# Late scatters of trees 1 and 2 issued during the FFN's first quads, with longer TensorE filler and earlier zero fills, in an attention + routed FFN kernel

## What is computed

```python
x = x + _L0_xattn_ref(_layernorm(x), ctx_1024, ctx_1024, w_q, w_k, w_v, w_o)
x = x + _L0_ffn_ref(_layernorm(x), ...)

def _fff(x, node_w, node_b, w1, b1, w2, b2):
    cur = jnp.zeros((N,), jnp.int32)
    for _ in range(DEPTH):                      # 4
        score = jnp.einsum('nd,nd->n', xf, node_w[cur]) + node_b[cur]
        cur = 2 * cur + 1 + (score >= 0).astype(jnp.int32)
    sel = jax.nn.one_hot(cur - N_NODES, N_LEAVES)      # 16 leaves
    hidden = relu(jnp.einsum('nd,ldh->lnh', xf, w1) + b1[:, None, :]) * sel.T[:, :, None]
    return jnp.einsum('lnh,lho->no', hidden, w2) + sel @ b2

q = _fff(x, q_...); k = _fff(x, k_...); v = _fff(x, v_...)
attn = softmax(einsum('bqd,bkd->bqk', q, k) / sqrt(256));  return attn @ v
```

## Time and profile before

| | |
|---|---|
| median of 3 runs | 658.25 us (657.19 to 658.79) |
| span of the profiled execution | 692.2 us |
| granted TensorE clock, mean | 0.941 |
| TensorE busy | 602.4 us, 87% |
| VectorE, ScalarE, GpSimd busy | 437.1, 297.2, 236.4 us |
| DMA | 173.78 MB, 251 GB/s on average |
| scatters (96 indirect DMAs) | 95.5 us busy, 995 ns each |
| first quad's transposes start | 440.77 us |
| last `copy_y` of the FFN starts | 601.25 us |

### The profile page before, as it was taken

One profiled execution on the slowest core, in us unless ns is written; L12 is line 12 of the kernel. 1 busy time (PEld: TensorE's weight loads), 2 busy tenths in 40 slices (PEclk: granted clock), 3 DMA queues, 4 the chain that ended last, 5 costly groups with the idle time before them and its releaser, 6 DMA issues.

```text
span 692.2 us, 14814 instructions
## 1 busy us (share of the span) xinstructions
PE 602.4 (87%) x5131; PEld 501.3 (72%) x5131; DVE 437.1 (63%) x1511; ACT 297.2 (43%) x482; POOL 236.4 (34%) x298
## 2 busy tenths in 40 slices
PE   7668999998998999999989766699968879787997
PEld 6556888887777878887778556588736747676995
DVE  3854677888788888898888746544403423154664
ACT  4114454454444444454444420277625625632322
POOL 5700011332422333234232435400266264355341
PEclk9869999999999999999999988599969978999999
DMA  6897989899989999999884887599958977755552
GB/s 191 254 304 226 276 260 256 262 274 284 290 241 286 299 264 275 292 298 288 242 273 141 275 244 184 190 325 340 395 174 291 340 245 248 255 162 170 167 172 87
DMA packets 105015, 173.78 MB, mean 251 GB/s; under 512 B 14128, under 2 KB 73200, under 8 KB 104944
## 3 DMA queue, kind: packets, MB, share of 16 engines
q1 hardware_dynamic: 93088, 146.03, 67.7%
q0 software_dynamic: 9216, 25.18, 11.8%
q10 hardware_dynamic: 2640, 1.65, 0.9%
HBM read 92.59 MB, written 79.69 MB: 249 GB/s over the span
## 4 chain that ended last, share of the span: by engine, by line
PE 40%; DMA 18%; SPq 15%; issue 12%; DVE 6%; another core or an unknown queue 4%; ACT 4%; ACTq 1%; POOL 0%; DVEq 0%; POOLq 0%
DMA parts_dram<-k_lo 9%; SPq L330 7%; DMA parts_dram<-q_hi 6%; PE banks L819 5%; PE banks L808 5%; PE banks L834 5%; PE banks L876 3%; PE banks L897 3%; PE banks L539 3%; PE banks L524 3%; SPq L316 2%; PE banks L551 2%; DMA k<-parts_dram 2%; PE banks L865 2%
## 5 line engine op out<-in xcount | busy, mean ns | idle before, releaser
L1526 POOL DMA_INDIRECT xs_dram<-xn2s,place x96 | 95.5, 995 | 174.8 <-ACT pt L928 144.6
L928 ACT ACTIVATE pt<-banks 128x768 f32<-128x768 f32 x128 | 103.5, 810 | 114.3 <-PE banks L552 92.9
L1166 DVE TENSOR_REDUCE mneg<-banks 128x2 f32<-128x512 f32 x240 | 121.8, 549 | 48.3 <-PE banks L540 42.6
L539 PE MATMUL banks<-k,q 107*128 107x256 f32 x240 | 76.1, 368 | 22.3 <-DMA k<-parts_dram 12.8
L551 PE MATMUL banks<-q,k 109*128 109x256 f32 x256 | 74.1, 341 | 2.0 <-DMA q<-m_lo 0.3
L539 PEld LDWEIGHTS banks<-k,q 107*128 107x128 f32 x240 | 46.2, 193 | 33.9 <-DMA k<-parts_dram 17.4
L1383 DVE COPY wb<-tables 128x128 f32 x96 | 21.4, 223 | 73.2 <-remote 44.4
L567 PE MATMUL banks<-pt,vp 128*32 128x256 f32 (+1 forms) x1024 | 56.8, 341 | 5.4 <-ACT pt L928 5.4
L552 PE MATMUL banks<-q,k 109*128 109x128 f32 x256 | 57.5, 224 | 0.0
L808 PE MATMUL banks<-ident,xb 128*128 128x128 f32 x288 | 42.8, 295 | 14.2 <-issue 11.0
L540 PE MATMUL banks<-k,q 107*128 107x128 f32 x240 | 54.2, 226 | 0.0
(11 more groups left out here) (177 smaller groups left out, 1301.8 us busy)
## 6 DMA issues: line engine op xcount, KB each, us to landing
ys_dram<-yb SPq DMA_DIRECT2D x36, 512.0 KB
xb<-xs_dram SPq DMA_DIRECT2D x35, 512.0 KB
k<-parts_dram SPq DMA_DIRECT2D x128, 128.0 KB
q<-parts_dram SPq DMA_DIRECT2D x128, 128.0 KB
xs_dram<-zero SPq DMA_DIRECT2D x45, 256.0 KB
parts_dram<-q_hi SPq DMA_DIRECT2D x32, 256.0 KB
xs_dram<-zero SPq DMA_DIRECT2D x18, 384.0 KB, 4.5
tables<-leafw SPq DMA_DIRECT2D x16, 257.0 KB
```

The lines of the kernel that those rows point to most:

```text
L539: mm(ps[:, 0:S], q[0:KN, t, P:S], k[0:KN, t, :], start=True, stop=True)
L928: nc.scalar.activation(pt[:, 2 * p:2 * p + 2, :], st_banks(b, p)[:, :, 0:S + P], ACT.Exp, scale=SC).then_inc(exp_sb, 1)
L1166: last = nc.vector.tensor_reduce(mneg[1 - u][:, t, 2 * j:2 * j + 2], S_BANKS[:, :, cols], axis=AX.X, op=ALU.max, negate=True)
L1526: gp.indirect_dma_start(xs_dram[tree], bass.IndirectOffsetOnAxis(ap=place[:, k:k + 1], axis=0), xn2s[m % RING][:, t, :], None).then_inc(sc ...
```

## The change

- Batch 11's six scatters are issued one at a time in step 15, at the slots of `SLOTS`, each behind one more exponential (counts 119 to 124). Batch 12's into tree 0 comes at j = 7 of step 15, those of batches 13, 14 and 15 into tree 0 at j = 2 of steps 16, 17 and 18.
- The 16 indirect DMAs of batches 12 to 15 into trees 1 and 2 are issued after the pipeline, one about every two thirds of a quad, tied in turn to `xbT_ps`, `y_ps` and `h_ps`, from quad 0 to quad 10. GpSimd then waits that they have landed, ahead of its gathers. SP waits for tree 1's before it loads quad 12 and for tree 2's before quad 24.
- Since the ring has three slots, batch 15's normalised rows go to `vp[0]`, which attention no longer uses; VectorE waits for `pv_ps` there in place of batch 12's scatters.
- The zero fills 16, 17 and 18 are issued in step 15 straight after that of 15, twelve DMAs in a row, and counted in `zeroed_last`.
- The filler between the leaf matmul and `block_T(0)` has 90 matmuls for 24.

Only the last filler's count differs. The diff:

```diff
@@ -192,7 +192,7 @@
         ident_ok, ones_ok, wq_in, wk_in = (sem(n) for n in "ident_ok ones_ok wq_in wk_in".split())
         wt_late = sems("wt_late", TREES)
         x_in, c_in, xr_in = sems("x_in"), sems("c_in"), sems("xr_in")
-        zeroed_first, zeroed = sem("zeroed_first"), sems("zeroed")
+        zeroed_first, zeroed, zeroed_last = sem("zeroed_first"), sems("zeroed"), sem("zeroed_last")
         (stats1, aggr1, var1, rstd1, xn_done, xnT_ps, xnT_sb, q_ps, qh_sb, ql_sb, k_ps, kh_sb, kl_sb,
          v_ps, v_sb, s_ps, max_sb, mT_ps, mh_sb, ml_sb, st_ps, exp_sb, pv_ps, nd_sb, ndT_ps, rden_sb, a_sb, aT_ps, aT_sb,
          wo_ps, x1_sb, stats2, aggr2, var2, rstd2, xn2_sb, xn2T_ps, xn2T_sb, node_ps, sc_sb,
@@ -254,6 +254,12 @@
 
             eng.wait_ge(scat[tree][m % RING], 16 * T * (m // RING + 1))
 
+        def xn2_rows(m):
+
+            if m < NB - 1:
+                return xn2s[m % RING]
+            return vp[0][:].rearrange("p t h c -> p (t h c)")[:, 0:T * D].rearrange("p (t d) -> p t d", t=T)
+
         def lag(b):
 
             return LAG + 1 if b < NB - 1 else LAG
@@ -276,7 +282,7 @@
 
         NCONST = 3
         WARM, FILL, FILL_K, FILL_X = 36, 6, 24, 8
-        IDLE = 14, 24, 30, 8, 16, 70, 24
+        IDLE = 14, 24, 30, 8, 16, 70, 90
         NALC = 11
 
         S_BANKS, ST_BANKS, W_BANKS, G6, G7 = pairs[0], pairs[1], banks[4:6], banks[6], banks[7]
@@ -333,15 +339,10 @@
             def zero_pages(b):
 
                 k = 3 if b <= 3 else 2
-                done = zeroed_first if b <= 3 else zeroed[b % 2]
+                done = zeroed_first if b <= 3 else zeroed_last if b >= NB else zeroed[b % 2]
                 for tree in range(TREES):
                     sp.dma_start(by_page(xs_dram[tree])[:, zero_from(b):zero_from(b + 1), :],
                                  zero[:, 0:k * D].rearrange("p (r d) -> p r d", d=D)).then_inc(done, 16)
-
-            def zero_after(b):
-
-                sp.wait_ge(zeroed[b % 2], 16 * TREES * ((b - 4) // 2))
-                zero_pages(b)
 
             def load_table(t, k):
 
@@ -377,10 +378,11 @@
                     stack(b + 1, 1 - u, 3)
                 if has(b, 2):
                     unload(b + 2, n + 1, u, 0)
-                if b <= NB:
+                if b < NB:
                     zero_pages(b)
-                if b == NB + 1:
-                    zero_after(b + 1)
+                if b == NB - 1:
+                    for late in (NB, NB + 1, NB + 2):
+                        zero_pages(late)
                 if has(b, -1):
                     load_xr(b - 1, 1 - u)
                 if has(b, -2):
@@ -409,8 +411,6 @@
                         sp.wait_ge(st_ps, PAIRS * (NB - 1))
                         for k in range(2):
                             load_table(1 if b <= NB else 2, (b - NB + 1) % 2 * 2 + k)
-                    if b == NB:
-                        zero_after(b + 1)
 
             def ramp():
                 for b in range(2):
@@ -455,6 +455,9 @@
 
             def load_quad(q):
 
+                if q % QUADB == 0:
+                    for m in range(NB - RING, NB):
+                        scattered(sp, q // QUADB, m)
                 ge(sp, xbT_ps, q - QB + 1)
                 rows = quad_rows(xs_dram[q // QUADB], q % QUADB)
                 if q == 0:
@@ -468,16 +471,10 @@
                 sp.wait_ge(y_sb, q + 1)
                 sp.dma_start(quad_rows(ys_dram[q // QUADB], q % QUADB), yb[q % QB][:]).then_inc(y_out[q % QB], 16)
 
-            sp.wait_ge(zeroed[0], 16 * TREES * 8)
-            sp.wait_ge(zeroed[1], 16 * TREES * 7)
-            for m in range(NB - RING, NB):
-                scattered(sp, 0, m)
-            for q in range(QB):
-                load_quad(q)
-            for tree in range(1, TREES):
-                for m in range(NB - RING, NB):
-                    scattered(sp, tree, m)
-            for q in range(QB, QB + AHEAD):
+            sp.wait_ge(zeroed[0], 16 * TREES * 6)
+            sp.wait_ge(zeroed[1], 16 * TREES * 6)
+            sp.wait_ge(zeroed_last, 16 * TREES * 3)
+            for q in range(QB + AHEAD):
                 load_quad(q)
             for q in range(TREES * QUADB):
                 if q + QB + AHEAD < TREES * QUADB:
@@ -655,7 +652,7 @@
                         for t in range(T):
                             for c in range(C):
                                 last = nc.tensor.transpose(G6[:, c * S + t * P:c * S + t * P + P],
-                                                           xn2s[(b - 2) % RING][:, t, c * P:c * P + P], ident[:])
+                                                           xn2_rows(b - 2)[:, t, c * P:c * P + P], ident[:])
                         last.then_inc(xn2T_ps, 1)
                         if b == NB + 1:
                             warm(IDLE[3])
@@ -1179,11 +1176,13 @@
 
                         v.wait_ge(rstd2, b - 1)
                         ge(v, xn2T_ps, b - 3)
-                        if b - 2 >= RING:
+                        if b - 2 == NB - 1:
+                            v.wait_ge(pv_ps, 4 * (NB - 1))
+                        elif b - 2 >= RING:
                             for r in range(TREES):
                                 scattered(v, r, b - 2 - RING)
                         for t in range(T):
-                            nc.vector.tensor_scalar(xn2s[(b - 2) % RING][:, t, :], x1[u][:, t, :], mv2[:, t, 0:1],
+                            nc.vector.tensor_scalar(xn2_rows(b - 2)[:, t, :], x1[u][:, t, :], mv2[:, t, 0:1],
                                                     rs2[:, t:t + 1], ALU.subtract, ALU.mult).then_inc(xn2_sb, 1)
                     if j == 5 and has(b, -1):
                         divide(b, 1)
@@ -1518,35 +1517,32 @@
 
                 if m == 0:
                     gp.wait_ge(zeroed_first, 16 * TREES * 6)
+                elif m + 3 >= NB:
+                    gp.wait_ge(zeroed_last, 16 * TREES * 3)
                 else:
                     gp.wait_ge(zeroed[(m + 3) % 2], 16 * TREES * ((m + 1) // 2))
                 gp.wait_ge(alloc, al(m, NAL))
                 for t in ts:
                     k = (m * T + t) * TREES + tree
                     gp.indirect_dma_start(xs_dram[tree], bass.IndirectOffsetOnAxis(ap=place[:, k:k + 1], axis=0),
-                                          xn2s[m % RING][:, t, :], None).then_inc(scat[tree][m % RING], 16)
+                                          xn2_rows(m)[:, t, :], None).then_inc(scat[tree][m % RING], 16)
 
             def step(b, n, u):
                 for j in range(PAIRS):
                     if j in SLOTS and has(b, -4) and b < NB - 1:
                         gp.wait_ge(exp_sb, PAIRS * (b - 1) + j + (LAG + 2 if j < LAG else LAG + 1))
                         scatter(b - 4, SLOTS.index(j) // T, (SLOTS.index(j) % T,))
+                    if j in SLOTS and b == NB - 1:
+                        gp.wait_ge(exp_sb, PAIRS * b - 1 + SLOTS.index(j))
+                        scatter(b - 4, SLOTS.index(j) // T, (SLOTS.index(j) % T,))
                     if j == 1 and has(b, -2):
                         rsqrt(b - 2, aggr2, mv2, ve2, var2, rs2, rstd2, (xn2_sb, T * (b - 2)))
                     if j == 2 and b >= NB:
-                        for m, tree in LAST_SCATTERS[b - NB]:
-                            scatter(m, tree)
+                        scatter(b - 3, 0)
                     if j == 4 and has(b, 3):
                         rsqrt(b + 3, aggr1, mv1, ve1, var1, rs1, rstd1, (xn_done, T * (b + 3)))
-                    if j == 6 and b == NB - 1:
-                        for tree in range(TREES):
-                            scatter(b - 4, tree)
-                        for tree in range(TREES - 1):
-                            scatter(b - 3, tree)
-
-            LAST_SCATTERS = (((NB - 4, 2), (NB - 3, 0)),
-                             ((NB - 3, 1), (NB - 3, 2), (NB - 2, 0), (NB - 2, 1)),
-                             ((NB - 1, 0), (NB - 2, 2), (NB - 1, 1), (NB - 1, 2)))
+                    if j == 7 and b == NB - 1:
+                        scatter(b - 3, 0)
 
             def ramp():
                 rsqrt(0, aggr1, mv1, ve1, var1, rs1, rstd1, (xn_done, 0))
@@ -1576,6 +1572,20 @@
 
             ramp()
             pipeline(step)
+
+            late = [(m, tree, t) for tree in range(1, TREES) for m in range(NB - RING - 1, NB) for t in range(T)]
+            for n, (m, tree, t) in enumerate(late):
+                q, third = 2 * n // 3, 2 * n % 3
+                if third == 0:
+                    gp.wait_ge(xbT_ps, q + 2)
+                elif third == 1:
+                    gp.wait_ge(h_ps, q + 1)
+                else:
+                    gp.wait_ge(y_ps, q + 1)
+                scatter(m, tree, (t,))
+            for tree in range(1, TREES):
+                for m in range(NB - RING, NB):
+                    scattered(gp, tree, m)
 
             for s in range(2):
                 gp.wait_ge(x1_out[s], 16 * (NB // 2))
```

## The result

The changed kernel took **660.49 us** (median of 19 runs, 654.75 to 667.11) beside 657.1 us before (19 runs): ratio 1.0079, interval 1.0054 to 1.0105. I had forecast 653.9 and a range of 649 to 660. It is slower, by 5.2 us (0.79% of 657.1).

A forecast was written before the change was run, and what follows sets the result against it. TensorE was taken to bound the FFN, so only the one-batch-deep seam chain, with low clock and pauses, could pay: 2.5 + 0.5 - 2.0 + 1.5 + 1.9 = 4.4 us off 658.25, giving 653.9, range 649 to 660.

The forecast's parts named there:

- The share of the pauses: Engine pauses beside rows of GpSimd's indirect DMAs: net 12.4 us gained when profiled, 0.15 of it, 1.9, when timed.
- Rival 1: The pauses are real in timed runs too, so the whole 12.4 us counts: 643.4 us; chance 0.08.
- Rival 2: About half the pauses are real, the profiled span also holding some 6 us no timed run has: 650.4 us; chance 0.10.
- `rsqrt(13)` behind two scatters: Step 15: two of batch 11's scatters ahead of `rsqrt(13)` in GpSimd's queue delay `xn2s`; 2.0 us lost.
- `rsqrt(14)` freed: Attention: `rsqrt(14)` no longer stands behind two more scatters; up to 2.4 us, taken as 1.5 gained.
- The filler: Before the first quad: 90 matmuls keep TensorE's clock high for quads 0 and 1's transposes and `block_h(0)`; 2.5 us gained.
- Rival 3: The filler buys nothing, the clock not having fallen or the 90 overshooting: say 657.3 us; chance 0.22.
- Scatters out of the seam: Seam: one or two scatters fewer lie ahead of the first quad's load; 0.5 us gained, bounds 0 to 0.7.
- 16 scatters in the FFN: Quads 0 to 10: 5.9 us of DMA work, covered by 6.4 us of ring slack; taken 0, bound 5.9.
- rival 4: The FFN becomes bound by its transfers, stores or loads landing late: slower, 661.7 us; chance 0.14.
- Zero fills: Step 15: 9 more fills on SP's queue ahead of `xr(14)` and the tables; taken 0, 1 without cover.
- My four terms beside the pauses: Filler 2.5, scatters out of the seam 0.5, `rsqrt(13)` -2.0, `rsqrt(14)` 1.5: together 2.5 us gained.

The follow-up runs named there:

- a_warm24: Changed kernel with the last filler at 24 matmuls instead of 90: 661.54 us, ratio 1.0085 to the kernel before.
- a_seam2: Changed kernel with the 16 late scatters of batches 12 to 15 back in the seam: 661.7 us, ratio 1.0104 to the kernel before (656 to 655 us kind).
- b_again2: Kernel before, unchanged, run again where it takes 655 to 657 us: 655.7 us.
- after: Profiled execution of the changed kernel, nothing else altered: span 657.5 us, time 659.62 us.
- a_again: Changed kernel, unchanged, run again where the kernel before takes 655 to 657 us: 660.65 us, ratio 1.0088 to the kernel before.
- a_wide: Changed kernel with the 90 filler matmuls of 128 columns replaced by 23 of 512 columns: 660.98 us, ratio 1.0079 to the kernel before.
- b_again: Kernel before, unchanged, run again where it takes 700 to 702 us: 704.0 us, ratio 1.0054 against itself.

## Why the prediction was wrong

I had a gain of 4.4 us; the traces beside the times show a loss of 5.9. Of the 10.3 between them 5.0 are the path from the filler to the first `copy_y`, 2.0 the scatters in the FFN, 1.9 the pauses and 1.5 the clock in step 15. The filler's term failed most in size, that of the pauses in kind.

**The share of the pauses (+1.9).** I subtracted the median of the runs from the profiled time, found 33.95 us, and read it as pauses that timed runs mostly lack, a share of 0.15. There is no share. Where the times beside the change were taken there are none, and the gain is 0; where the profile was taken, timed runs have them whole, and the change gains 8.6 us. Rival 1 put the right question, whether timed runs have them, but took the two numbers to be of one condition. With the pauses whole I had 14.9 us (2.5 and 12.4) for all terms together: measured 7.6 or 10.3 in the seam, by the two traces of before, less 2.7 in the FFN, and the profiled run of that condition spans 693.2 us, not 677.3. If the other terms cost there the 3.9 that they cost in the 655 seam, the seam's pauses were worth 11.5 to 14.2 (an estimate), not 16.1. Why a row of scatters goes with them is open.

Rival 2 leant on the Trainium skill, Runtime: NRT & Kernel Launch, "The ~15µs preamble/postamble breakdown", where a profile's total stands 6.2 us above the reported time. Here the time stands 2.1 us above the span (659.62 and 657.5).

**`rsqrt(13)` behind two scatters (-2.0).** The wait is exactly that, 1.07 to 3.05. What I left out is the clock behind it: in 388 to 394 it was granted 0.54, the transposes took 1.08 and not 0.63, and 119 to 128 lost 3.4 to 3.6. In a_warm24 and a_seam2 they waited as long but took 0.63, and it lost 2.3 and 2.0. So the term is 2.0 and up to 1.6 for the clock, which doesn't fall in every run.

**`rsqrt(14)` freed (+1.5).** Right: 1.6. VectorE's wait for `rs` ahead of `xn2s(14)` is 2.47 us in b_again2, 0.21 in the changed kernel, and 2.46 again in a_seam2, where the scatters are back.

**The filler (+2.5).** Wrong. I looked at the wait of `block_T(0)` only. With a warm TensorE `block_T(1)` is next in line, and it waits for the second quad and starts 5.9 to 7.7 us behind SP's first load. The clock doesn't last that long: the granted clock fell to 0.50 in the wait for the first quad in a_seam2, at the end of its transposes in after and a_again, and in the wait for the second in the other three, so that `block_T(1)` took 1.94 to 1.97 us in all six. What is late next I had not asked. And I costed only the filler's time, not its 132 added instructions: 1.3 to 2.1 us more to the load (5.02 to 5.82 us for 3.75 to 3.79) by the fetched block, in every trace with 90 and in none with 24 or with 23 wide ones. Rival 3 had the gain of nothing, not the loss.

**Scatters out of the seam (+0.5).** 0: the load stands 3.75 us behind the scatter with them and 3.77 without.

**16 scatters in the FFN (0, bound 5.9).** -1.7 to -2.3 in the changed kernel in the 655 condition (-4.1 in a_wide). I had compared landings with a ring of four quads. The wait that counts is in the diff: `load_quad(12)` waits for tree 1's scatters, and SP reaches it behind quad 5's store, not at quad 12. This was rival 4's mechanism in part, transfers that land late; its 661.7 came near the result by other sums. GpSimd itself was not held up: the 16 late scatters took 0.95 to 1.18 us each in after. The 3100 ns that I weighed for one was no price for this case: a copy into `wb` takes 226 ns on average, so being shut out for the length of one could not add 2.5 us.

**Zero fills (0, bound 1).** 0 in the changed kernel, for the reason I named, but only because `rsqrt(13)` is late: with that repaired they cost 1.9 (23.8 against 21.9). Without that cover they cost at each of the three places tried in place of those of before: `xr` late by 1.7 and 2.0 us, and 8.3 us of waits for `k`.

Sum in the 655 condition: about -3.5 + 1.6 - 1.5 - 0.5 - 2.0 = -5.9, where the 0.5 is within the spread of that stretch; measured -5.2 and -5.8. No single term is clear of the noise in the times. My four terms beside the pauses had it at +2.5.

## What to carry to other kernels

Compare a profile with timed runs of its own execution first: if they are 5% apart, ask which condition each is of before any share is put on a stall, since a change can win in one and lose in the other. A wait in an in-order queue counts from where the queue reaches it, here six quads ahead of its use. Added filler is also added instructions, and work taken off one late operation pays only up to the next that is late.

## What the runs showed of the hardware

One kernel took 655 to 657 or 700 to 702 us, the difference being waits without a shown cause beside rows of GpSimd's indirect DMAs: VectorE's longest were 13.7 us in b_again, and TensorE was busy 36.16 of 50 us with gathers beside it, or 50.00 of 50 (b_again2) with more of them. What switches this was not found.

A 16.4 KB block of TensorE's instructions beside a scatter of 48 packets held three of them up (a_again), and the load behind it by 1.3 to 2.1 us in 11 traces; so 66 matmuls that only fill an idle stretch can lengthen the path through the memory.
